# Head reciprocals spread by DMA through DRAM, score maxima turned by VectorE, in an attention and mixture-of-experts kernel

## The chip, the cores and the metric

The kernel runs on one core of one Trainium2 chip. The metric is the device time of one execution in microseconds. Five engines work in parallel, each on its own instruction stream in program order: TensorE (PE in the profile; its weight loads are listed as PEld), VectorE (DVE), ScalarE (ACT), GpSimd (POOL) and SyncE (SP), which here issues most DMA transfers. They wait for each other through semaphores only.

## The reference

One transformer block on `x` of 4 batches x 512 tokens x 128, in fp32. The first half is attention with 16 query heads of 64 and one shared key/value head:

```
x  = layernorm(x) ; xn = layernorm(x, g1, b1)
q  = (xn @ Wq).reshape(b, n, 16, 64) * 64**-0.5 ; k, v = split(xn @ Wkv)
attn = softmax(q @ k.T) ; out = attn @ v
x  = x_in + layernorm(out.reshape(b, n, 1024) @ Wo, g2, b2)
```

The second half is a mixture of 8 experts (two for each token, softmax gate, GELU with gating, hidden width 512), whose result is added to `x`.

## The kernel before

The program has two blocks. In the first, attention runs in 8 units of 8 heads (two units to a batch). `attention_schedule` writes one list of steps, each with a slot number; every engine walks the same list and issues what is its own. A slot is one `EXP` step: 128 keys by 512 queries of one head, so a head has 4 slots, a unit 32 and the whole attention 256.

- `MAX`: TensorE multiplies 128 queries by all 512 keys into one of two banks of `max_ps` (L1209), and VectorE takes the row maximum into `rowmax` (L1058). TensorE may write a bank again only when VectorE has read it: product k waits for maximum k-2.
- `SHIFT`, 17 times, mostly for 4 heads at once: the maxima must lie along the queries of one row. TensorE turns them with four transposes (L1216), ScalarE copies them with a factor of -1 into `mrow` (L1107), and two DMAs put them in row 64 of `q_hm` (L905). The step stands 5 slots ahead of the first `EXP` that needs it, at slots 11 and 27 of each unit (the first two heads apart).
- `EXP`: two products into `s_ps` (L1238, L1240; the second adds the negated maxima) and ScalarE's exponential into `prob` (L1134). `PV` (L1254) multiplies `prob` by `v`, 4 slots to a head, two heads at a time.
- The sum of each head: GpSimd adds its four `prob` tiles in two instructions, `fold` (L989, 128x1024) and `psums` (L995, 128x512), as soon as the head's last `EXP` is done. GpSimd also copies queries to `q_hm` (L969).
- After a unit: TensorE sums over the partitions into `sum_ps` (`SUM`, L787), ScalarE copies (`SUMS`), a DMA spreads the sums on 128 partitions (`SPREAD`), VectorE takes the reciprocals (`RECIP`, L718) and splits them in a high and a low part (L721, L722), two DMAs gather these into 16 rows of `rhl` (`GATHER`, L750). Then, for each of the 4 pairs of heads, `NORM`: TensorE multiplies a constant, `headsel`, by `rhl` (L797), which repeats each head's reciprocals on its 64 partitions of `sum_ps`, and VectorE multiplies that by `raw`, the unnormalized output, into `ao` (L731). `OUT` multiplies by `Wo` (L807). `NORM` stands at slots 14, 17, 19 and 22 of the next unit.

The second block does the experts. It opens with the last unit's `SPREAD` to `OUT`, mixed with the first expert tiles, while GpSimd sends rows to DRAM (L489) and then forms the low parts of the weights (L1356, `wl`).

Of the kernel before, what the change touches and what calls it, by code (L numbers as in the profile page):

```python
# [24 lines left out]
LOW_ROW = 32  # L25


def attention_schedule(units):
# [51 lines left out]
    for u in range(units):  # L80
        after = slots * (u + 1)
        if u < units - 1:
# [4 lines left out]
            for c in range(UP):  # L87
                place(after + NORM_AT[c], 5, "NORM", u, c)
                place(after + NORM_AT[c] + OUT_LAG, 5, "OUT", u, c)
# [28 lines left out]

SUM_AT = (-7, 5)
# [4 lines left out]
LAST_STEPS = (("SUMS", 0), ("SPREAD", 0), ("RECIP", 0), ("GATHER", 0), ("NORM", 0), ("NORM", 1), ("OUT", 0),  # L124
# [54 lines left out]
def bass_preln_mqa_moe_kernel(nc, x, ln1_g, ln1_b, wq, wkv, wo, ln2_g, ln2_b, gate_wT, gate_upT, downT,  # L179
# [16 lines left out]
    parts = nc.dram_tensor("parts", [TOP_K * T, P], F32).ap()  # L196

# [12 lines left out]
    with ExitStack() as whole:  # L210
# [64 lines left out]
        headsel = sb(whole, "headsel", [P, UP, P], F32R)  # L275
# [3 lines left out]
        halves = sb(whole, "halves", [P, 2, SPREAD], F32R)  # L279
        rhl = sb(whole, "rhl", [P, S], F32R)  # L280
# [403 lines left out]
        def load_rows(sp, k, dst):  # L684
# [49 lines left out]
        def tail_sync(sp, kind, u):  # L734
# [42 lines left out]
        def tail_tensor(pe, kind, u, a):  # L777

            b = u // 2
            if kind == "SUM":  # L780
                k = 2 * u + a
                sums_done(pe, 4 * (k + 1))
                if a == 0 and u >= 1:

                    pe.wait_ge(ao_ready, u * UP)
# [26 lines left out]
        tail_steps = [step for step in steps[last_pv:] if step[0] in ("RAW", *RECIP_STEPS, "NORM", "OUT")]  # L812
# [3 lines left out]
        with ExitStack() as att:  # L816
# [18 lines left out]
            rowmax = sb(att, "rowmax", [P, 2, TPB, 4])  # L835
            mrow = sb(att, "mrow", [4, 2, S], F32R)
# [11 lines left out]
            hs_raw = raw[:, RAW_SLOTS - 1, :].rearrange("p (u n) -> p u n", n=P)  # L848
# [16 lines left out]
            def shift_bank(n):  # L865


                return sum_ps if n == 0 else q_ps

# [3 lines left out]
            def _(sp):  # L873
# [10 lines left out]
                for half in range(2):  # L884
                    for part in range(2):
                        row = part * LOW_ROW + half * UH // 2
                        sp.dma_start(hs_raw[row:row + UH // 2, :, :],
                                     head_rows[half + 2 * part:P:32, :, :]).then_inc(hs_in, 16)
# [5 lines left out]
                for kind, u, a in steps:  # L894
                    tail_sync(sp, kind, u)
                    if kind == "SHIFT":
# [6 lines left out]
                        for h in range(0, heads, 2):  # L903
                            slot = (head + h) % Q_SLOTS
                            sp.dma_start(q_hm[DH:DH + 1, slot:slot + 2, :].bitcast(F32),  # L905
                                         mrow[h:h + 2, u % 2, :].bitcast(F32)).then_inc(mrow_in[u % 2], 16)
# [16 lines left out]
            def _(pool):  # L923
# [27 lines left out]
                for kind, u, a in steps:  # L951
# [12 lines left out]
                    if kind == "Q":  # L964
# [6 lines left out]
                        if k == 0:  # L971
                            link_pool(pool, nc.gpsimd.memset(headsel[:, :, :].bitcast(F32), 0.0))
# [758 lines left out]
```

## Time and profile before

| | us |
|---|---|
| median of 3 runs | 621.6 (621.18 to 623.62) |
| profiled execution | 620.37 |
| its span | 618.6 |
| TensorE busy | 579.3 (94%) |
| VectorE busy | 388.5 (63%) |
| GpSimd busy | 395.4 (64%) |
| ScalarE busy | 307.1 (50%) |

The span runs from the first to the last instruction that the profile shows; the execution's own time is 1.8 us more. Busy times of matmuls are modelled and overlap, so a busy TensorE is judged by the start times of its instructions. The granted clock of TensorE is a fraction of its full speed.

### The profile page before, as it was taken

Reading aid. Unit: us, or ns where it says so; the run is one execution under the profiler, and the core shown is the slowest. Engines: PE = TensorE matmul, PEld = TensorE weight load, DVE = VectorE, ACT = ScalarE, POOL = GpSimd, SP = SyncE. Lnnn points to the kernel's source line nnn. Section 1 sums busy time; section 2 is a strip of 40 time slices with the busy share of each in tenths; the row PEclk is TensorE's granted clock in tenths of the full one; section 3 lists DMA queues with packets and bytes.
Section 4 is the critical chain, followed back from the end, with each engine's and each line's share of the span. In section 5 each row is a group of like instructions: output and inputs, shape, how many; then the busy total and the mean of one; then the engine's idle time right before and its main releaser. Section 6 shows DMA issues by size and latency. Waiting matters only on the chain. (4 is left out here: it accounts for less than half of the span.)

```text
span 618.6 us, 8866 instructions
## 1 busy us (share of the span) xinstructions
PE 579.3 (94%) x2611; PEld 330.1 (53%) x2611; DVE 388.5 (63%) x792; ACT 307.1 (50%) x576; POOL 395.4 (64%) x329
## 2 busy tenths in 40 slices
PE   8799999999999998998999989999997979999990
PEld 6464555444554454454545535444443567888880
DVE  4967557656646878584567786975384468444443
ACT  2345646455546554463556445545635553455540
POOL 5457677658668855598598558959745934354331
PEclk9999999999999999798999999999999999999996
DMA  5111012010101200061000000000004400230005
GB/s 162 69 70 70 2 70 73 1 69 3 72 24 48 73 0 2 6 229 76 2 2 3 1 2 17 23 1 2 12 1 123 118 22 27 67 94 29 21 16 204
DMA packets 26990, 29.46 MB, mean 48 GB/s; under 512 B 7523, under 2 KB 18021, under 8 KB 26944
## 3 DMA queue, kind: packets, MB, share of 16 engines
q1 hardware_dynamic: 24672, 24.66, 12.3%
q0 software_dynamic: 2272, 4.24, 2.1%
q8 instruction: 23, 0.38, 0.3%
q14 instruction: 23, 0.19, 0.1%
HBM read 13.50 MB, written 15.32 MB: 47 GB/s over the span
## 5 line engine op out<-in xcount | busy, mean ns | idle before, releaser
L1134 ACT ACTIVATE prob<-s_ps 128x512 f32<-128x512 f32 x256 | 150.5, 598 | 177.0 <-PE s_ps L1240 175.1
L1058 DVE TENSOR_REDUCE rowmax<-max_ps 128x1 f32<-128x512 f32 x256 | 174.2, 690 | 101.4 <-PE max_ps L1209 99.1
L989 POOL TENSOR_TENSOR fold<-prob 128x1024 f32<-128x1024 f32 x63 | 149.8, 2377 | 94.5 <-ACT prob L1134 93.9
L1254 PE MATMUL pv_ps<-prob,v 128*64 128x512 f32 x512 | 139.0, 623 | 0.0
L1238 PE MATMUL s_ps<-q_hl,khh 128*128 128x512 f32 x256 | 118.5, 463 | 0.6 <-ACT prob L1134 0.6
L1209 PE MATMUL max_ps<-khh,q_hl 128*128 128x512 f32 x256 | 103.3, 409 | 7.7 <-DVE rowmax L1058 3.9
L1240 PE MATMUL s_ps<-q_hm,kly 65*128 65x512 f32 x256 | 102.3, 400 | 0.0
L1238 PEld LDWEIGHTS s_ps<-q_hl,khh 128*128 128x128 f32 x256 | 48.9, 191 | 79.5 <-ACT prob L1134 59.8
L995 POOL TENSOR_TENSOR psums<-fold 128x512 f32<-128x512 f32 x63 | 82.3, 1306 | 4.9
L1209 PEld LDWEIGHTS max_ps<-khh,q_hl 128*128 128x128 f32 x256 | 49.1, 192 | 27.3 <-DVE rowmax L1058 11.2
L1240 PEld LDWEIGHTS s_ps<-q_hm,kly 65*128 65x128 f32 x256 | 49.0, 191 | 8.9 <-issue 3.4
L1254 PEld LDWEIGHTS pv_ps<-prob,v 128*64 128x64 f32 x512 | 25.6, 135 | 46.1 <-issue 34.9
L489 POOL DMA_INDIRECT sorted_rows<-xr,place_i x32 | 34.2, 1068 | 21.4 <-issue 11.8
L1047 DVE TENSOR_TENSOR q_hl<-q_ps,q_hl 64x512 fp32r<-64x512 f32 x64 | 44.1, 689 | 5.9 <-ACT q_hl L1116 4.6
L1442 DVE TENSOR_TENSOR ha<-up_ps,gl 128x512 f32<-128x512 f32 x39 | 26.9, 690 | 30.8 <-PE up_ps L1569 22.7
L1591 PE MATMUL sum_ps<-wd,ht 128*128 x312 | 41.9, 277 | 4.3 <-DVE raw L1451 3.9
L1116 ACT ACTIVATE q_hl<-q_ps 64x512 fp32r<-64x512 f32 x64 | 37.6, 588 | 7.8 <-PE q_ps L1146 7.0
L1591 PEld LDWEIGHTS sum_ps<-wd,ht 128*128 128x128 f32 x312 | 37.9, 192 | 5.9 <-issue 5.9
L1403 POOL DMA_INDIRECT parts<-raw,psums x22 | 21.4, 973 | 30.3 <-DVE raw L1451 25.4
L731 DVE TENSOR_TENSOR ao<-sum_ps,raw 128x512 f32<-128x512 f32 x32 | 22.1, 691 | 28.9 <-PE sum_ps L797 28.9
L969 POOL TENSOR_SCALAR q_hm<-q_hl 64x1024 fp32r<-64x1024 f32 x32 | 33.4, 1044 | 6.7 <-ACT q_hl L1116 6.7
L1510 ACT ACTIVATE ht<-q_ps 128x512 f32<-128x512 f32 x39 | 23.3, 597 | 24.4 <-PE q_ps L1578 24.4
(230 smaller groups left out, 767.2 us busy)
## 6 DMA issues: line engine op xcount, KB each, us to landing
sorted_rows<-raw_w SPq DMA_DIRECT2D x36, 260.0 KB, 2.6
raw_w<-in_gate_upT SPq DMA_DIRECT2D x8, 512.0 KB, 8.3
wd<-in_downT SPq DMA_DIRECT2D x8, 256.0 KB
raw_w<-parts SPq DMA_DIRECT2D x8, 256.0 KB, 3.9
psums<-sorted_rows SPq DMA_DIRECT2D x22, 65.0 KB, 1.9
x<-in_x SPq DMA_DIRECT2D x4, 256.0 KB, 4.1
out<-x SPq DMA_DIRECT2D x4, 256.0 KB, 2.3
xs_first<-sorted_rows SPq DMA_DIRECT2D x15, 65.0 KB, 2.2
```

What stands on the lines that cost most here:

```text
L489: nc.gpsimd.indirect_dma_start(out=sorted_rows, out_offset=bass.IndirectOffsetOnAxis(ap=place_i[:, n, t:t + 1], axis=0), in_=xr[:, n, t, : ...
L989: nc.gpsimd.tensor_tensor(fold[:, :, :], prob[:, head % 4, 0:2, :], prob[:, head % 4, 2:4, :], ALU.add).then_inc(prob_folded, 1)
L995: nc.gpsimd.tensor_tensor(psums[:, head % SUM_SLOTS, :], fold[:, 0, :], fold[:, 1, :], ALU.add).then_inc(head_sum, 1)
L1047: nc.vector.tensor_tensor(q_hl[DH:P, h % Q_SLOTS, :], q_ps[DH * hd:DH * hd + DH, :], q_hl[0:DH, h % Q_SLOTS, :].bitcast(F32), ALU.subtract ...
L1058: nc.vector.tensor_reduce(rowmax[:, group % 2, it, i:i + 1], max_ps[:, k % 2, :], AX_X, ALU.max).then_inc(max_done, 1)
L1116: nc.scalar.activation(q_hl[0:DH, (2 * k + hd) % Q_SLOTS, :], q_ps[DH * hd:DH * hd + DH, :], ACT.Copy).then_inc(q_hi, 1)
L1134: nc.scalar.activation(prob[:, head % 4, jt, :], s_ps[:, k % 2, :], ACT.Exp, scale=SCALE).then_inc(exp_done, 1)
L1209: nc.tensor.matmul(max_ps[:, k % 2, :], q_hl[:, k // JT % Q_SLOTS, it * P:(it + 1) * P], khh[:, b % 2, :], start=True, stop=True).then_inc ...
L1238: nc.tensor.matmul(s_ps[:, k % 2, :], khh[:, b % 2, keys], q_hl[:, slot, :], start=True, stop=False)
L1240: nc.tensor.matmul(s_ps[:, k % 2, :], kly[0:DH + 1, b % 2, keys], q_hm[0:DH + 1, slot, :], start=False, stop=True).then_inc(score_mm, 1)
L1254: last = nc.tensor.matmul(pv_ps[DH * hd:DH * hd + DH, :], v[:, b % 2, jt, :], prob[:, head % 4, jt, :], start=(jt == 0), stop=(jt == JT - 1))
L1591: last = nc.tensor.matmul(down_ps[:, :], ht[:, k % 2, c * P:(c + 1) * P], wd[:, weights(k, DN, c * P, P)], start=c == 0, stop=c == FC - 1)
```

## The change

- `NORM` loses its product. `GATHER` writes the 128x32 reciprocals to a DRAM tensor, `recips`. Four new steps `CAST`, at slots 10.5, 10.5, 12 and 12, wait until that write has landed and read two heads' rows back, each row 64 times, into `over_sum`, which lies in SBUF (256 KB each). VectorE's `NORM` multiplies `over_sum` by `raw`, so that both of its inputs now lie in SBUF. The split in high and low parts, `headsel`, `rhl` and GpSimd's preparation of them go.
- `SHIFT` loses its transposes and ScalarE's copy. VectorE multiplies the maxima by -1 into `less_max` (128x16) and turns it with four 32x32 transposes into `mrow`. The two DMAs stay.
- In the second block, four `CAST` DMAs stand behind all loads of `wd`, and VectorE's four `NORM` behind the second `hidden`; the products that keep TensorE busy at the start of the block read other data.

```diff
             if kind == "RECIP":
                 dve.wait_ge(spread_in, 32 * (u + 1))
-                link(dve, nc.vector.reciprocal(rinv[:, :], spread[:, :]))
                 if u >= 1:
-                    dve.wait_ge(rhl_in, 32 * u)
-                link(dve, nc.vector.tensor_copy(halves[:, 0, :], rinv[:, :]))
-                nc.vector.tensor_tensor(halves[:, 1, :], rinv[:, :], halves[:, 0, :].bitcast(F32),
-                                        ALU.subtract).then_inc(recip_done, 1)
+                    dve.wait_ge(recips_out, 16 * u)
+                nc.vector.reciprocal(rinv[:, :], spread[:, :]).then_inc(recip_done, 1)
             if kind == "NORM":
                 k = u * UP + a
-                dve.wait_ge(norm_mm, k + 1)
+                dve.wait_ge(over_sum_in[a], 16 * (u + 1))
                 dve.wait_ge(raw_ready, k + 1)
...
-                nc.vector.tensor_tensor(ao[:, k % 2, :], sum_ps[:, :], raw[:, k % RAW_SLOTS, :],
+                nc.vector.tensor_tensor(ao[:, k % 2, :], over_sum[:, a, :], raw[:, k % RAW_SLOTS, :],
                                         ALU.mult).then_inc(ao_ready, 1)
...
             if kind == "GATHER":
                 sp.wait_ge(recip_done, u + 1)
+                sp.dma_start(recips[u].rearrange("(p c) -> p c", c=SPREAD), rinv[:, :]).then_inc(recips_out, 16)
+            if kind == "CAST":
+                sp.wait_ge(recips_out, 16 * (u + 1))
                 if u >= 1:
-                    sp.wait_ge(norm_mm, u * UP)
-                else:
-                    sp.wait_ge(consts_set, 1)
-                for part in range(2):
-                    sp.dma_start(rhl[part * LOW_ROW:part * LOW_ROW + UH, :].bitcast(F32),
-                                 halves[:, part, :].bitcast(F32)).then_inc(rhl_in, 16)
+                    sp.wait_ge(ao_ready, (u - 1) * UP + a + 1)
+                of_pair = recips[u, 2 * a * S:2 * (a + 1) * S].rearrange("(h q) -> h q", h=2)
+                sp.dma_start(over_sum[:, a, :],
+                             of_pair.unsqueeze(1).broadcast_to([2, DH, S])).then_inc(over_sum_in[a], 16)
...
-            if kind == "NORM":
-                k = u * UP + a
-                pe.wait_ge(rhl_in, 32 * (u + 1))
-                if k >= 1:
-                    pe.wait_ge(ao_ready, k)
-                nc.tensor.matmul(sum_ps[:, :], headsel[:, a, :], rhl[:, :], start=True,
-                                 stop=True).then_inc(norm_mm, 1)
...
+                    if kind == "SHIFT":
+                        head, heads = shift_heads[u]
+                        group, i = divmod(head, 4)
+                        cols = slice(i * JT, (i + heads) * JT)
+                        dve.wait_ge(max_done, (head + heads) * JT)
+                        if u >= 2:
+
+                            rows_came(dve, u - 2)
+                        link(dve, nc.vector.tensor_scalar(less_max[:, u % 2, cols], rowmax[:, group % 2, cols], -1.0, None,
+                                                          ALU.mult))
+                        for n in range(P // 32):
+                            part = slice(32 * n, 32 * n + 32)
+                            last = nc.vector.transpose(mrow[:, u % 2, part].bitcast(F32),
+                                                       less_max[part, u % 2, :].bitcast(F32))
+                        last.then_inc(mrow_ready, 1)
...
-                    if kind == "SHIFT":
-                        head, heads = shift_heads[u]
-                        pe.wait_ge(max_done, (head + heads) * JT)
-                        group, i = divmod(head, 4)
-                        for t in range(TPB):
-                            last = nc.tensor.transpose(shift_bank(u)[0:heads, t * P:(t + 1) * P],
-                                                       rowmax[:, group % 2, t, i:i + heads],
-                                                       ident[:, :])
-                        last.then_inc(shift_mm, 1)
```

On VectorE, early in the second unit, the kernel before has from the reciprocals to the first two `NORM` (the names in a row are what is written and what is read; x5 means five in a row):

```order
L718 RECIPROCAL rinv<-spread 128x32
L721 CAST halves<-rinv 128x32
L722 TENSOR_TENSOR halves<-rinv,halves 128x32
L1058 TENSOR_REDUCE rowmax<-max_ps 128x1 x5
L731 TENSOR_TENSOR ao<-sum_ps,raw 128x512
L1058 TENSOR_REDUCE rowmax<-max_ps 128x1 x2
L1047 TENSOR_TENSOR q_hl<-q_ps,q_hl 64x512 x2
```

The changed kernel has there on VectorE:

```order
L724 RECIPROCAL rinv<-spread 128x32
L1038 TENSOR_REDUCE rowmax<-max_ps 128x1 x2
L1048 TENSOR_SCALAR less_max<-rowmax 128x16
L1052 STREAM_TRANSPOSE mrow<-less_max 32x32 x4
L1038 TENSOR_REDUCE rowmax<-max_ps 128x1 x3
L732 TENSOR_TENSOR ao<-over_sum,raw 128x512
```

The split has gone, five small instructions stand between the second and the third maximum, and `NORM` reads `over_sum` in place of a bank of PSUM.

In the middle of the attention, in the unit in which a later batch's statistics (BN) are also taken, VectorE has before:

```order
L722 TENSOR_TENSOR halves<-rinv,halves 128x32
L1058 TENSOR_REDUCE rowmax<-max_ps 128x1 x2
L361 BN_STATS stats<-x 128x6 x4
L364 BN_AGGR moments<-stats 128x2 x4
L1058 TENSOR_REDUCE rowmax<-max_ps 128x1 x3
```

and after the change:

```order
L1038 TENSOR_REDUCE rowmax<-max_ps 128x1 x2
L1048 TENSOR_SCALAR less_max<-rowmax 128x16
L1052 STREAM_TRANSPOSE mrow<-less_max 32x32 x4
L363 BN_STATS stats<-x 128x6 x4
L366 BN_AGGR moments<-stats 128x2 x4
L1038 TENSOR_REDUCE rowmax<-max_ps 128x1 x3
```

The five instructions and the statistics now stand one behind the other ahead of the same three maxima.

## Rows read from the trace of the kernel before

**Rows 1.** The page, busy us of each engine (share of the span), instructions.
```profile
PE 579.3 (94%) x2611; PEld 330.1 (53%) x2611; DVE 388.5 (63%) x792; ACT 307.1 (50%) x576; POOL 395.4 (64%) x329
```

**Rows 2.** Busy us by engine in one stretch; then granted clock, DMA share, GB/s.
```profile
100.00:160.00 60.00, 60.00 (x244) 29.60 (x243) 37.76 (x63) 32.89 (x61) 41.13 (x28) 1.00 0.15 56
```

**Rows 3.** Timeline of TensorE: start, duration, line, operation; modelled ends.
```profile
99.80 0.60 PE L1216 MATMUL q_ps<-ident,rowmax 128*4 128x128 f32 x4
...
100.47 0.40 PE L1240 MATMUL s_ps<-q_hm,kly 65*128 65x512 f32 x1
...
103.46 0.50 PE L797 MATMUL sum_ps<-rhl,headsel 128*128 128x512 f32 x1
...
104.03 0.39 PE L1240 MATMUL s_ps<-q_hm,kly 65*128 65x512 f32 x1
...
106.99 0.50 PE L1238 MATMUL s_ps<-q_hl,khh 128*128 128x512 f32 x1
107.32 0.40 PE L1240 MATMUL s_ps<-q_hm,kly 65*128 65x512 f32 x1
```

**Rows 4.** Timeline: small VectorE instructions beside GpSimd; brackets give idle time before, releaser.
```profile
236.78 1.32 POOL L995 TENSOR_TENSOR psums<-fold 128x512 f32<-128x512 f32 x1
...
237.61 0.53 DVE L580 TENSOR_SCALAR picked<-cnt 128x32 f32<-128x32 f32 x1
...
240.77 2.37 POOL L989 TENSOR_TENSOR fold<-prob 128x1024 f32<-128x1024 f32 x1 [2.67 <-ACT prob L1134]
...
241.06 2.17 DVE L594 TENSOR_TENSOR of_pick<-pick,pr 128x64 f32<-128x64 f32 x1
...
399.65 2.83 DVE L657 TENSOR_TENSOR tile_j<-places,tile_j 128x9 f32<-128x9 f32 x1
...
404.07 0.50 PE L1209 MATMUL max_ps<-khh,q_hl 128*128 128x512 f32 x1 [0.96 <-DVE rowmax L1058]
```

**Rows 5.** Timeline around two SHIFT steps, at slots 11 and 27 of a unit.
```profile
99.34 2.38 POOL L989 TENSOR_TENSOR fold<-prob 128x1024 f32<-128x1024 f32 x1 [1.13 <-ACT prob L1134]
...
101.13 2.12 DVE L1058 TENSOR_REDUCE rowmax<-max_ps 128x1 f32<-128x512 f32 x3 [1.46 <-PE max_ps L1209]
...
102.13 0.39 PE L1209 MATMUL max_ps<-khh,q_hl 128*128 128x512 f32 x1
...
129.12 2.12 DVE L1058 TENSOR_REDUCE rowmax<-max_ps 128x1 f32<-128x512 f32 x3 [2.41 <-PE max_ps L1209]
```

**Rows 6.** Timeline around a SHIFT step with statistics beside it.
```profile
205.90 2.38 POOL L989 TENSOR_TENSOR fold<-prob 128x1024 f32<-128x1024 f32 x1 [0.82 <-ACT prob L1134]
...
206.47 0.86 DVE L361 BATCH_NORM_STATS2 stats<-x 128x6 f32<-128x128 f32 x4
...
207.69 2.12 DVE L1058 TENSOR_REDUCE rowmax<-max_ps 128x1 f32<-128x512 f32 x3
...
208.70 0.39 PE L1209 MATMUL max_ps<-khh,q_hl 128*128 128x512 f32 x1
```

**Rows 7.** The first SHIFT step: timeline of VectorE and ScalarE.
```profile
21.44 1.41 DVE L1047 TENSOR_TENSOR q_hl<-q_ps,q_hl 64x512 fp32r<-64x512 f32 x2
...
22.10 0.59 ACT L1107 ACTIVATE mrow<-sum_ps 2x512 fp32r<-2x512 f32 x1 [1.92 <-PE sum_ps L1216]
```

**Rows 8.** VectorE's NORM instructions (ns min/median/max) and what they waited for (us, times).
```profile
L731 DVE TENSOR_TENSOR ao<-sum_ps,raw x32: 680/692/693, 104.0 to 480.9; 128x512 f32<-128x512 f32 x32
...
  PE sum_ps L797: 28.9, 27
```

**Rows 9.** Stretches with idle TensorE, and one behind it; columns as in rows 2.
```profile
245.40:248.90 3.50, 1.49 (x6) 0.78 (x8) 3.41 (x6) 1.19 (x2) 0.44 (x2) 1.00 0.00 0
249.00:255.80 6.80, 6.80 (x22) 2.88 (x18) 2.75 (x8) 1.68 (x3) 3.21 (x2) 0.50 0.00 0
...
363.00:366.50 3.50, 1.54 (x6) 0.67 (x4) 3.41 (x6) 1.20 (x2) 0.43 (x2) 1.00 0.00 0
```

**Rows 10.** The second block: GpSimd's low weight parts in the timeline.
```profile
480.24 13.44 POOL L1356 TENSOR_TENSOR wl<-raw_w,wh 128x512 fp32r<-128x512 f32 x10
```

More of the change, by code:

```diff
@@ L24 @@
 SPREAD = 32
-LOW_ROW = 32
 def attention_schedule(units):
@@ L87, in attention_schedule @@
             for c in range(UP):
+                place(after + CAST_AT[c], 5, "CAST", u, c)
                 place(after + NORM_AT[c], 5, "NORM", u, c)
@@ L811, in bass_preln_mqa_moe_kernel @@
         last_pv = max(n for n, step in enumerate(steps) if step[0] == "PV")
-        tail_steps = [step for step in steps[last_pv:] if step[0] in ("RAW", *RECIP_STEPS, "NORM", "OUT")]
+        tail_steps = [step for step in steps[last_pv:] if step[0] in ("RAW", *RECIP_STEPS, "CAST", "NORM", "OUT")]
         assert all(step in tail_steps or step[0] in ("PV", "SUM") for step in steps[last_pv:])
@@ L834, in bass_preln_mqa_moe_kernel @@
             wvl = sb(att, "wvl", [P, DH], F32R)
-            rowmax = sb(att, "rowmax", [P, 2, TPB, 4])
-            mrow = sb(att, "mrow", [4, 2, S], F32R)
+            rowmax = sb(att, "rowmax", [P, 2, 4 * JT])
+            less_max = sb(att, "less_max", [P, 2, 32], F32R)
+            mrow = sb(att, "mrow", [32, 2, P], F32R)
             prob = sb(att, "prob", [P, 4, JT, S])
@@ L971, in _ @@
                         if k == 0:
-                            link_pool(pool, nc.gpsimd.memset(headsel[:, :, :].bitcast(F32), 0.0))
-                            link_pool(pool, nc.gpsimd.memset(rhl[:, :].bitcast(F32), 0.0))
-                            pool.wait_ge(hs_in, 64)
-                            for part in range(2):
-                                held = slice(part * LOW_ROW, part * LOW_ROW + UH)
-                                nc.gpsimd.tensor_scalar(headsel[held, :, :], hs_raw[held, :, :], 1.0, 1.0, ALU.mult,
-                                                        ALU.mult).then_inc(headsel_set, 1)
-                                pool.wait_ge(headsel_set, part + 1)
                             set_constants(pool)
@@ L1168, in _ @@
                         keep_busy(BUSY[kind])
-                    if kind in ("XT", "K", "V", "Q", "SHIFT", "YT", "X3T", "LOGIT", "RANK") and (kind, u) not in (("K", 0), ("SHIFT", 0)):
+                    if kind in ("XT", "K", "V", "Q", "YT", "X3T", "LOGIT", "RANK") and (kind, u) != ("K", 0):
                         if in_bank:
@@ L1371, in load_down @@
                                  downT[e].rearrange("(c p) n -> p c n", p=P)).then_inc(wd_in, 16)
[L1373 to L1379 removed]
+                tail_sync(sp, "SPREAD", last_unit, 0)
+                load_down(0)
+                load_down(1)
+                load_rows(sp, EARLY_ROWS, rows(EARLY_ROWS))
+                tail_sync(sp, "GATHER", last_unit, 0)
+                for e in range(2, E):
+                    load_down(e)
+                for c in range(UP):
+                    tail_sync(sp, "CAST", last_unit, c)
+                for k in range(EARLY_ROWS + 1, LIST_TILES[0]):
                     load_rows(sp, k, rows(k))
@@ L1457, in _ @@
                 low_gate_up(dve, 1, wl_ready)
-                tail_vector(dve, "NORM", last_unit, 0)
                 low_gate_up(dve, 2, wl_ready)
-                tail_vector(dve, "NORM", last_unit, 1)
                 hidden(1)
-                tail_vector(dve, "NORM", last_unit, 2)
-                tail_vector(dve, "NORM", last_unit, 3)
+                for c in range(UP):
+                    tail_vector(dve, "NORM", last_unit, c)
                 hidden(2)
@@ L1616, in up, with keep_busy @@
                     times(up_ps[:, k % 2, :], k, F).then_inc(up_mm, 1)
-                def keep_busy(times):
-                    for _ in range(times):
-                        nc.tensor.matmul(ht_ps[:, :], headsel[:, 0, :], headsel[:, :, :].rearrange("p k c -> p (k c)"),
-                                         start=True, stop=True)
-                keep_busy(4)
+                def keep_busy(width):
+                    nc.tensor.matmul(ht_ps[:, 0:width], ident[:, :], wof[:, 0:width // P, :].rearrange("p k c -> p (k c)"),
+                                     start=True, stop=True)
+                keep_busy(S)
                 turn_in(0)
-                keep_busy(2)
+                keep_busy(S // 2)
                 for e in range(E):
```

80 lines of the change are left out of this document (28 added, 52 removed).

## The prediction

> **What bounds the kernel now.** I read the page first: TensorE is busy 94% of the span, VectorE 63%, GpSimd 64% [rows 1]. Busy times of matmuls overlap by model, so I then took the stretches: between 100 and 160 us TensorE is busy 60.00 of 60.00 us at the full clock, while VectorE has 37.8 and GpSimd 41.1 [rows 2]. The timeline says the same by start times: the products follow each other at fixed distances, whatever the others do. So in the attention (to about 465 us) each product taken out is worth its distance to the next, as long as nobody makes TensorE wait. What can make it wait is VectorE: product k into `max_ps` waits for maximum k-2. So the questions are what leaves TensorE, and what the five new instructions and the new inputs of `NORM` do to VectorE's queue.
>
> **What is removed.** Behind a `PV` the next score product's partner L1240 starts 0.33 us after its L1238 (107.32 less 106.99). With a `NORM` product in front, it starts 0.57 us after that product's start (104.03 less 103.46), so `NORM` costs TensorE 0.24 us; with the four transposes in front 0.67 us (100.47 less 99.80), so a `SHIFT` costs 0.34 us [rows 3]. In the attention there are 28 `NORM` (four more come in the second block) and 17 `SHIFT`: 28 x 0.24 + 17 x 0.34 = 6.7 + 5.8 = 12.5 us saved. ScalarE's copies, GpSimd's preparation of `headsel` and VectorE's split go too; these engines have idle time there, so I count them at nothing. If that cover were gone (VectorE late), the split would give back about what the `SHIFT` instructions take; it stands at another place, so it does not help there.
>
> **What is added on VectorE: a wait for GpSimd.** The trace shows small VectorE instructions with all inputs and outputs in SBUF that last as long as a GpSimd instruction beside them. A 128x32 TENSOR_SCALAR takes 0.53 us and ends at 238.14, just after GpSimd's `psums` addition (236.78 + 1.32 = 238.10); a 128x64 TENSOR_TENSOR takes 2.17 us and ends at 243.23, just after a `fold` (240.77 + 2.37 = 243.14) [rows 4]. The first has one SBUF input, as `less_max` has; the second has two, as `NORM` now has. Maxima and additions that read PSUM keep their length.
>
> Each `SHIFT` stands right behind the last maximum of slot 11 or 27, and `fold` follows the exponential of the same slot. At 99.80 the transposes could start, because the maximum was ready; `fold` had started at 99.34 and ran to 101.72 [rows 3, 5]. So `less_max` gets in 0.4 us too late and ends at about 101.76. I find this order, by 0.2 to 1.1 us, at eleven of the seventeen steps. The four transposes are not in the trace. From below they cost nothing beyond the wait; from above 0.69 us each, as a full 128x512 instruction [rows 8]. I take 0.15 us each, since a 32-column instruction is nearest to the small ones here, whose work behind a wait is under 0.1 us: 0.6 us, VectorE free at 102.37.
>
> Place by place, with the maximum at 0.69 us:
> - Slot 11, no statistics, `fold` ahead: three steps. VectorE had been idle 1.46 us and took its next maximum at 101.13. Now it ends at 102.37 + 0.69 = 103.06, and the product that waits for it started at 102.13 [rows 5]. TensorE stands 0.93 us past its old time, 1.27 us with the 0.34 saved: 3 x 1.27 = 3.8 us.
> - Slot 11 with statistics: two steps. `fold` ends at 208.28, the transposes at 208.9, the statistics (1.22 us from 206.47 to 207.69) at 210.15, the maximum at 210.84, where the product started at 208.70 [rows 6]: 2.14 + 0.34 = 2.5 us, twice: 5.0 us.
> - Slot 27, six steps. VectorE was idle 2.41 us there, a microsecond more [rows 5], so that 1.27 becomes about 0.35: 2.1 us.
> - The first step. `mrow` came at 22.10 + 0.59 = 22.69 from ScalarE; VectorE is busy until 22.85 and would deliver at about 23.6 [rows 7]. The first `EXP` waits for it: 0.9 us.
> - The remaining five: nothing.
>
> A case in the trace bears this out: a VectorE wait of 2.83 us for GpSimd cost TensorE a gap of 0.96 us soon after [rows 4].
>
> `NORM` is kinder. It no longer waits for TensorE, which was 28.9 us over 27 of them, 1.07 us each, and its own time stays near 0.69 us [rows 8]. Against that stands a wait of up to one `fold`, 2.4 us, when it meets one. Laid over GpSimd's instructions, most of the 28 come out no later than before, a few later by up to 1.2 us: 1.9 us of waits in all, bounds 0 and 28 x 1.2 = 34 us, the low value because VectorE has over a third of its time free [rows 2].
>
> Sum so far: -12.5 + 3.8 + 5.0 + 2.1 + 0.9 + 1.9 = +1.2 us. The saving is spent in VectorE's queue.
>
> **The clock.** From 245.4 to 248.9 TensorE was busy 1.49 of 3.5 us, and from 249.0 to 255.8 it was granted 0.50, its level of 1.2 GHz; a like gap from 363.0 to 366.5 left it at 1.00 [rows 9]. The two gaps of 2.5 us are of this kind. A 3.4 us stretch at half speed loses 1.7 us. Bounds: none, and four of them (6.8 us, as after 249). I take one, 1.7 us.
>
> **The DMAs.** SyncE's queue gets, per unit, one write, a wait for it and four transfers of 256 KB. `SHIFT`'s DMAs stand between the `CAST` pairs and depend on `mrow`, which is late by 1.3 us at slot 11. The step stands five slots ahead of the `EXP` that it serves, some 8 us at 440 us for 256 slots; `mrow` would be there 2.6 us after 99.80, and two issues and a transfer fit in the rest. I count nothing, and 1 us for each of seven at worst.
>
> **The second block.** The `CAST` transfers queue behind 2 MB of `wd`, and I estimate the four `NORM` at 479 to 484, where the last one began at 480.9 before [rows 8]. There GpSimd works through ten `wl` subtractions, 13.44 us without a pause from 480.24 [rows 10], on which the first tiles with split weights wait. If `NORM` holds GpSimd off as GpSimd holds VectorE, each costs it up to 0.69 us; bounds 0 and 2.8 us. I take 1.5 us. No row here shows GpSimd held off by VectorE. The Trainium skill (SBUF — State Buffer, Who interferes with whom) says that the two share a port pair as an exclusive lock which the one that starts first keeps for its whole instruction; by it the term would be 2.8 us when all four collide.
>
> **Sum.** +1.2 + 1.7 + 1.5 = +4.4 us on the profiled execution's 620.4, that is 624.8. The median is 1.2 us above that execution, so 621.6 + 4.4 = 626.0 us.
>
> One page speaks for the change. The Trainium skill (VectorE: DVE Perf Modes, Rules for kernel authors) calls VectorE's transpose the fastest for 32x32, and gives 311 ns for a 128x128 bf16 one. With 0.31 us for each of my four, five gaps would be 0.64 us longer and the forecast 629.
>
> **The rivals.** A measurement tells about 0.5% (3.1 us) from no change.
> 1. *My forecast*, waits at the `SHIFT` steps that spend the saving, chance 0.45: 626.0, own range 622 to 632.
> 2. *The saving mostly stays*, 0.24. `less_max` comes first. ScalarE no longer copies the maxima, and VectorE reaches the step 0.2 to 1.1 us behind `fold`'s start: if it gets there ahead of `fold` in most units, GpSimd waits instead, which has slack. Then 3.8 + 5.0 + 2.1 shrink to about 2 us, no clock is lost: 621.6 - 12.5 + 2 + 0.9 + 1.9 + 1.0 = 615. It decides when `fold` starts later than the end of the last maximum in over half of the units. For it speaks that six of seventeen steps already go this way; against it that the order follows from the step list, slot after slot. Should `NORM` cost nothing either, 612.
> 3. *It evens out*, 0.20: waits of half my size and no clock loss, -12.5 + 7 + 1.5 = -4, or with one loss -2: 618.5 to 623.
> 4. *Worse*, 0.11: each of the seven gaps at slot 11 costs the clock, 7 x 1.7 = 11.9 in place of 1.7, or the late `mrow` adds its 7 us: 633 to 636.
>
> **How the numbers follow.** Rival 4 (0.11) and the part of my own range above 624.7 (0.36 of 0.45) are slower by over 0.5%; rival 2 (0.24) and the low end of 3 (0.02) are faster, below 618.5. That gives slower 0.47, same 0.27, faster 0.26. The range for 8 in 10 cuts off the ends of rivals 2 and 4: 612 to 633.
>
> **What would show it.** TENSOR_SCALAR of `less_max` at a mean well over 1 us (a minimum near 0.17), its end at `fold`'s; TensorE idle before max_ps products, released by `rowmax`, 12 us or more in all; transposes at 0.1 to 0.2 us; `NORM` between 0.7 and 3 us; a granted clock of 0.5 in new places behind the longest gaps; `wl` over 14 us. It is wrong if `less_max` is short in most steps, if the transposes cost more than 0.3 us each, or if TensorE's first `EXP` of a unit waits for a DMA.

## The result, and the profile after

The changed kernel takes 720.81 us (median of 4 runs, 720.35 to 721.71) against 621.39 us: a ratio of 1.159, 95% interval 1.156 to 1.162. The forecast was 626.0 with a range of 612 to 633. The sign of the likeliest case was right; the size was wrong by 95 us. The reason for most of it had been priced at 7 us at worst, in rival 4.

The page of the changed kernel, the lines that answer to [rows 1] and the groups with the largest waits:

```profile
PE 603.9 (84%) x2509; PEld 332.3 (46%) x2509; DVE 422.7 (59%) x862; ACT 298.0 (41%) x559; POOL 395.2 (55%) x325
...
L1215 PE MATMUL s_ps<-q_hl,khh 128*128 128x512 f32 x256 | 133.5, 521 | 44.8 <-DMA q_hm<-mrow 44.1
...
L1195 PE MATMUL max_ps<-khh,q_hl 128*128 128x512 f32 x256 | 108.1, 428 | 20.6 <-DVE rowmax L1038 16.8
...
L802 PE MATMUL y_ps<-ao,wof 128*128 128x512 f32 x64 | 41.6, 736 | 19.2 <-DVE ao L732 19.2
```

TensorE's share falls from 94% to 84%. It stands 44.1 us before `EXP` products because the maxima's rows (`q_hm<-mrow`) have not landed, 19.2 us before `OUT`, and 16.8 us before `MAX` products. The last is what the prediction was about. The first was its last condition for being wrong. The waits give how often (us in total, times, longest):

```profile
DVE ao L732 <- DMA over_sum<-recips: 45.3, 11, 10.6
PE s_ps L1215 <- DMA q_hm<-mrow: 44.1, 7, 9.1
...
PE y_ps L802 <- DVE ao L732: 19.2, 4, 9.9
...
PE max_ps L1195 <- DVE rowmax L1038: 16.8, 18, 2.7
```

One of the seven, in the timeline of the changed kernel from 100 us (SPq rows are SyncE's DMA issues: start, and how long the issuing took). It is the place of [rows 3] and [rows 5]:

```profile
101.90 1.11 SPq L752 DMA_DIRECT2D over_sum<-recips  x2
102.14 2.39 POOL L967 TENSOR_TENSOR fold<-prob 128x1024 f32<-128x1024 f32 x1 [1.14 <-ACT prob L1120]
102.31 2.25 DVE L1048 TENSOR_SCALAR less_max<-rowmax 128x16 fp32r<-128x16 f32 x1
...
104.60 0.84 DVE L1052 STREAM_TRANSPOSE mrow<-less_max 32x32 f32<-32x32 f32 x4
...
105.47 1.42 SPq L891 DMA_DIRECT2D q_hm<-mrow  x2
106.16 0.47 PE L1195 MATMUL max_ps<-khh,q_hl 128*128 128x512 f32 x1 [1.40 <-DVE rowmax L1038]
...
108.89 5.90 SPq L752 DMA_DIRECT2D over_sum<-recips  x2
...
115.37 0.79 PE L1215 MATMUL s_ps<-q_hl,khh 128*128 128x512 f32 x1 [6.14 <-DMA q_hm<-mrow]
```

Two things are to be seen. `less_max` starts 0.17 us behind `fold` and ends with it (104.56 and 104.53): the wait that I forecast, with the gap that I forecast (1.40 us, forecast 1.27). And two transfers of 4 KB, issued at 105.47 with two of 256 KB in flight before them, have landed only when the product starts at 115.37. What the DMA engines do meanwhile is in the windows of the same stretch (columns: PE, PEld, DVE, ACT and POOL busy, granted clock, mean share of the 16 DMA engines, GB/s):

```profile
104.00:106.00 2.00, 0.76 (x4) 0.30 (x2) 1.93 (x7) 1.44 (x3) 1.83 (x2) 1.00 0.13 51
...
108.00:110.00 2.00, 1.23 (x6) 0.66 (x4) 0.56 (x1) 0.60 (x1) 0.98 (x1) 1.00 1.05 395
...
112.00:114.00 2.00, 0.00 (x0) 0.00 (x0) 0.50 (x1) 0.00 (x0) 1.02 (x1) 0.75 0.13 43
114.00:116.00 2.00, 0.63 (x2) 0.53 (x3) 0.00 (x0) 0.00 (x0) 0.00 (x0) 0.50 0.13 49
116.00:118.00 2.00, 2.00 (x7) 0.59 (x5) 0.91 (x2) 1.35 (x3) 0.00 (x0) 0.50 0.13 50
```

With nothing but `CAST` in flight, the share is 0.13, which is 2 of 16, at 43 to 51 GB/s, while the same engines reach 395 GB/s between 108 and 110, when the loads of rows run. At 50 GB/s each 256 KB takes 5 us, and a unit has four. TensorE meanwhile drops to its lower clock (0.50, 1.2 GHz) and stays there into the work.

The 19.2 us ahead of `OUT` all lie in the second block, where TensorE takes up the four pairs of heads as their `CAST` transfers come in, 4.6 to 5.7 us apart:

```profile
564.45 2.08 PE L802 MATMUL y_ps<-ao,wof 128*128 128x512 f32 x2 [9.95 <-DVE ao L732]
570.14 2.08 PE L802 MATMUL y_ps<-ao,wof 128*128 128x512 f32 x2 [3.61 <-DVE ao L732]
574.76 2.08 PE L802 MATMUL y_ps<-ao,wof 128*128 128x512 f32 x2 [2.54 <-DVE ao L732]
579.90 2.08 PE L802 MATMUL y_ps<-ao,wof 128*128 128x512 f32 x2 [3.06 <-DVE ao L732]
```

### The profile page after: what moved, and what is told of

Its sections match the earlier page's. It is cut to its first block and busy times, and to the rows that moved or that the text cites. A ratio compares the mean times of both kernels' runs of the same rounds, so it can differ in the third digit from the quotient of the medians.

```text
span 719.2 us, 8703 instructions
## 1 busy us (share of the span) xinstructions
PE 603.9 (84%) x2509; PEld 332.3 (46%) x2509; DVE 422.7 (59%) x862; ACT 298.0 (41%) x559; POOL 395.2 (55%) x325
## 5 line engine op out<-in xcount | busy, mean ns | idle before, releaser
L1215 PE MATMUL s_ps<-q_hl,khh 128*128 128x512 f32 x256 | 133.5, 521 | 44.8 <-DMA q_hm<-mrow 44.1
L1231 PE MATMUL pv_ps<-prob,v 128*64 128x512 f32 x512 | 150.0, 668 | 0.0
L1195 PE MATMUL max_ps<-khh,q_hl 128*128 128x512 f32 x256 | 108.1, 428 | 20.6 <-DVE rowmax L1038 16.8
L1215 PEld LDWEIGHTS s_ps<-q_hl,khh 128*128 128x128 f32 x256 | 51.6, 202 | 153.7 <-ACT prob L1120 62.2
L1217 PE MATMUL s_ps<-q_hm,kly 65*128 65x512 f32 x256 | 107.1, 418 | 0.0
L973 POOL TENSOR_TENSOR psums<-fold 128x512 f32<-128x512 f32 x63 | 83.8, 1331 | 4.9
L1195 PEld LDWEIGHTS max_ps<-khh,q_hl 128*128 128x128 f32 x256 | 52.0, 203 | 45.3 <-issue 17.8
L732 DVE TENSOR_TENSOR ao<-over_sum,raw 128x512 f32<-128x512 f32 x32 | 30.3, 946 | 64.6 <-DMA over_sum<-recips 45.3
L1217 PEld LDWEIGHTS s_ps<-q_hm,kly 65*128 65x128 f32 x256 | 52.4, 205 | 11.7 <-issue 7.2
L802 PE MATMUL y_ps<-ao,wof 128*128 128x512 f32 x64 | 41.6, 736 | 19.2 <-DVE ao L732 19.2
L1231 PEld LDWEIGHTS pv_ps<-prob,v 128*64 128x64 f32 x512 | 26.8, 142 | 48.4 <-issue 37.8
L1026 DVE TENSOR_TENSOR q_hl<-q_ps,q_hl 64x512 fp32r<-64x512 f32 x64 | 44.1, 690 | 5.6 <-ACT q_hl L1103 4.1
L1103 ACT ACTIVATE q_hl<-q_ps 64x512 fp32r<-64x512 f32 x64 | 37.6, 587 | 12.5 <-PE q_ps L1132 11.6
```

The lines of the kernel that those rows point to most:

```text
L802: nc.tensor.matmul(y_ps[:, :], wof[:, c, :], ao[:, k % 2, :], start=c == 0, stop=c == PAIRS - 1).then_inc(out_mm, 1)
L973: nc.gpsimd.tensor_tensor(psums[:, head % SUM_SLOTS, :], fold[:, 0, :], fold[:, 1, :], ALU.add).then_inc(head_sum, 1)
L1026: nc.vector.tensor_tensor(q_hl[DH:P, h % Q_SLOTS, :], q_ps[DH * hd:DH * hd + DH, :], q_hl[0:DH, h % Q_SLOTS, :].bitcast(F32), ALU.subtract ...
L1103: nc.scalar.activation(q_hl[0:DH, (2 * k + hd) % Q_SLOTS, :], q_ps[DH * hd:DH * hd + DH, :], ACT.Copy).then_inc(q_hi, 1)
L1195: nc.tensor.matmul(max_ps[:, k % 2, :], q_hl[:, k // JT % Q_SLOTS, it * P:(it + 1) * P], khh[:, b % 2, :], start=True, stop=True).then_inc ...
L1215: nc.tensor.matmul(s_ps[:, k % 2, :], khh[:, b % 2, keys], q_hl[:, slot, :], start=True, stop=False)
```

## The experiments

Theory A was that two DMA engines carry each `CAST`. e1 to e3 test it; the question after them was what the two halves of the change cost by themselves, and e4 to e10 take them apart. The runs stand in the order of the argument. A difference between two kernels that ran beside different runs of the kernel before is good to about 3 us.

### e1: each CAST in two transfers

```diff
-                of_pair = recips[u, 2 * a * S:2 * (a + 1) * S].rearrange("(h q) -> h q", h=2)
-                sp.dma_start(over_sum[:, a, :],
-                             of_pair.unsqueeze(1).broadcast_to([2, DH, S])).then_inc(over_sum_in[a], 16)
+                for h in range(2):
+                    row = recips[u, (2 * a + h) * S:(2 * a + h + 1) * S].rearrange("(o q) -> o q", o=1)
+                    sp.dma_start(over_sum[h * DH:(h + 1) * DH, a, :],
+                                 row.broadcast_to([DH, S])).then_inc(over_sum_in[a], 16)
```

> Each CAST is made as two transfers, one for each head, whose pattern is 64 rows by 512 in place of 2 by 64 by 512; the bytes, the repeated row and all else stay. Theory A (the pattern with an outer dimension of 2 is carried by two of the sixteen DMA engines, share 0.13, so a 256 KB transfer takes 5 us, and the mrow transfers wait behind two of them): the DMA share during a CAST rises towards 1, TensorE's 44 us of waiting for q_hm<-mrow falls under 3 us, VectorE's 45 us for over_sum<-recips under 5 us, and the time comes to 626 us, what the prediction's other terms give. Theory B (reading one DRAM row 64 times is slow in itself): the time stays within 10 us of 720.

647.1 us, ratio 1.040 (1.032 to 1.049): 74 us come back by the shape of a transfer that moves the same bytes. Its windows have, for the same stretch:

```profile
104.00:106.00 2.00, 0.60 (x4) 0.20 (x3) 1.93 (x7) 1.26 (x3) 1.65 (x2) 1.00 0.54 168
```

And the answer on its tile `over_sum`:

```profile
DMA to landing us min/median/max: 2.7/3.0/4.8
```

Each half lands 3.0 us after its issue (median), TensorE's wait for `q_hm<-mrow` falls from 44.1 to 1.2 us, and four issues of `CAST` at 108.70 take 2.54 us where two took 5.90. A share of 0.13 could also be sixteen engines that are each busy an eighth of the time; the packets in the two traces speak against that. In both kernels a packet is a row of 2,048 bytes and mostly takes 84 ns. From 104.0 to 105.4 us the changed kernel never has fewer than two in flight, at 90% of the moments exactly two and else three; e1 has 6 to 17 (104.0 to 105.2). Theory A holds for the cause. Two of its numbers were missed: VectorE's wait for `over_sum` fell from 45.3 only to 10.0 us (expected under 5), and the time is 21 us above the 626 expected. Those 21 us are what e4 to e10 are about.

### e2: the same pattern, 128 different rows

```diff
-                             of_pair.unsqueeze(1).broadcast_to([2, DH, S])).then_inc(over_sum_in[a], 16)
+                sp.dma_start(over_sum[:, a, :].bitcast(F32), gate_upT[0:2, 0:DH, 0:S]).then_inc(over_sum_in[a], 16)
```

> Each CAST keeps its pattern of 2 by 64 by 512 but reads 128 different rows of the gate/up weights in place of two rows 64 times each; so over_sum holds other numbers, and the output is not the reference's. Theory A (the pattern decides): 720 us within 8, DMA share 0.13 during a CAST. Theory B (the repeated row decides): about 626 us.

717.0 us in one run, and the waits of the changed kernel:

```profile
DVE ao L732 <- DMA over_sum<-in_gate_upT: 47.4, 11, 10.0
PE s_ps L1213 <- DMA q_hm<-mrow: 45.6, 7, 9.6
```

That one row is read 64 times makes no difference that this one run shows. The pattern does it.

### e3: the maxima's rows ahead of all CAST

```diff
-CAST_AT = (10.5, 10.5, 12, 12)
+CAST_AT = (11.5, 11.5, 12, 12)
```

> The first two CAST steps move from slot 10.5 to 11.5, so that SyncE issues the mrow transfers of slot 11 ahead of all four CAST. Theory A with a queue in order: TensorE's wait for q_hm<-mrow falls from 44 us to under 10 us, the waits for over_sum stay or grow (the same 20 us of transfers for each unit, begun 4 us later), and the time falls by 20 to 40 us, to 680 to 700. If the slow transfers hold up the mrow rows whatever the order (the engines share them out), the time stays within 8 us of 720.

713.6 us in one run; I had expected 680 to 700. The wait for `mrow` has gone, and comes back in other rows of its waits:

```profile
DVE ao L732 <- DMA over_sum<-recips: 114.5, 27, 11.3
...
PE max_ps L1195 <- DVE rowmax L1038: 53.5, 26, 8.4
```

VectorE now stands in `NORM`, its maxima behind it, and TensorE waits for those (53.5 us, 16.8 in the changed kernel). Where the slow transfers stand in the queue hardly matters: 20 us of them per unit collide with one thing or another.

### e5: only VectorE's turn, NORM as before

The kernel before, with `SHIFT` of the changed kernel (`less_max` and four transposes in place of TensorE's transposes and ScalarE's copy) and nothing else.

> The kernel before with only the second part of the change: the maxima are negated and turned on VectorE; NORM keeps its product and the gather of before. The prediction's terms for this part: -5.8 us for the transposes, +3.8, +5.0, +2.1 and +0.9 us of waits, one loss of clock of 1.7 us: 621.4 + 7.7 = 629 us, range 622 to 634, less_max at a mean near 1.4 us. Rival (VectorE has room for it, the waits for GpSimd cost TensorE nothing): 621.4 - 5.8 = 615.6 us.

638.3 us, ratio 1.024 (1.016 to 1.031). Its `less_max` by duration (ns, least/median/longest):

```profile
L1072 DVE TENSOR_SCALAR less_max<-rowmax x17: 158/1720/2294, 21.8 to 449.6; 128x16 fp32r<-128x16 f32 x15, 128x8 fp32r<-128x8 f32 x2
```

TensorE's largest wait in it, which is 3.9 us in the kernel before:

```profile
PE max_ps L1220 <- DVE rowmax L1062: 17.1, 17, 2.7
```

And its windows at two gaps and behind three (PE busy, granted clock, DMA share, GB/s):

```profile
212.00:216.00 4.00, 1.38 (x6) 1.00 0.03 5
...
217.10:220.50 3.40, 3.40 (x10) 0.50 0.65 242
...
336.60:343.40 6.80, 6.05 (x13) 0.50 0.01 1
377.00:380.90 3.90, 1.77 (x7) 1.00 0.00 0
380.90:387.70 6.80, 6.80 (x24) 0.50 0.00 0
```

This half of the change alone costs 17 us (638.3 less 621.5, the kernel before beside it), where 7.7 were expected. The gaps are those of the prediction: 1.40 us three times, 2.72 twice, about 0.5 at four later steps. The clock is not: the mean granted clock is 0.962 (before 0.980). Half clock stands behind one of the three gaps of 1.40 us (3.4 us from 53.3 us on) and behind both of 2.72 (3.4 and 6.8 us). The 6.8 us from 380.9 on follow no gap of the change. They follow the one that [rows 9] shows from 363.0 on, where TensorE waits for VectorE's part in the choice of experts, and behind which the clock stayed at 1.00 before. Why it falls here and not there stays open.

### e7: the turn one slot earlier

```diff
-        place(FIRST_SHIFT_AT[n] if n < 2 else JT * head - lead + 1, 3, "SHIFT", n, 0)
+        place(FIRST_SHIFT_AT[n] if n < 2 else JT * head - lead, 3, "SHIFT", n, 0)
```

> The kernel of e5 (before, with the maxima turned on VectorE) with each SHIFT but the first two one slot earlier, at slots 10 and 26, so that less_max reaches VectorE before the fold of slot 11 or 27 has started. Theory (the time of e5 is less_max waiting for fold, the gaps that this makes on TensorE, and the clock lost behind them): less_max at a mean under 0.6 us in place of 1.34, TensorE's gaps before max_ps near the 8 us of before in place of 21, half clock near 27 us in place of 51, and 617 us, range 614 to 622. Rival (the five instructions cost this much wherever they stand): 632 or more.

637.6 us, ratio 1.030 (1.027 to 1.033): a miss. `less_max` did get ahead of `fold`, in 14 of 17 steps (the median is 165 ns):

```profile
L1072 DVE TENSOR_SCALAR less_max<-rowmax x17: 158/165/2324, 22.3 to 447.2; 128x16 fp32r<-128x16 f32 x15, 128x8 fp32r<-128x8 f32 x2
```

But two of the three that still wait are those ahead of the statistics, where the gaps are longest. One of them in the timeline of VectorE:

```profile
204.06 2.32 DVE L1072 TENSOR_SCALAR less_max<-rowmax 128x16 fp32r<-128x16 f32 x1
...
207.86 0.87 DVE L361 BATCH_NORM_STATS2 stats<-x 128x6 f32<-128x128 f32 x4
```

The windows of TensorE behind four gaps of the same kernel (columns as for e5):

```profile
209.00:216.00 7.00, 6.13 (x13) 0.51 0.41 154
...
253.00:260.00 7.00, 6.54 (x19) 0.54 0.01 2
...
332.00:339.00 7.00, 6.03 (x15) 0.51 0.01 1
376.00:386.00 10.00, 9.52 (x28) 0.52 0.00 0
```

Only the first and third of these stretches stand behind a wait of `less_max` ahead of statistics. The second is there in the kernel before too (249.0 to 255.8, [rows 9]); the fourth follows the gap that cost no clock before, as at 380.9 in e5. So taking the wait from most steps hardly moves the time: TensorE's wait for `rowmax` falls from 17.1 to 13.8 us, and the clock's loss stays near that of e5.

### e8: no negation, so no waiting instruction

```diff
-            less_max = sb(att, "less_max", [P, 2, 32], F32R)
...
-                        link(dve, nc.vector.tensor_scalar(less_max[:, u % 2, cols], rowmax[:, group % 2, cols], -1.0, None,
-                                                          ALU.mult))
...
-                nc.vector.memset(kly[DH:DH + 1, :, :].bitcast(F32), 1.0).then_inc(ones_set, 1)
+                nc.vector.memset(kly[DH:DH + 1, :, :].bitcast(F32), -1.0).then_inc(ones_set, 1)
```

e5, where the transposes read `rowmax` itself and the sign comes from the constant row of `kly` that multiplies it.

> The kernel of e5 without less_max: the maxima are turned as they are, straight from rowmax, and the row of ones in kly holds -1 in place of 1, so that the product subtracts them. It computes the same. Theory (the one instruction with the shared port waits; the transposes do not): TensorE's gaps before max_ps within 3 us of before's 8, and 617 us, range 614 to 622. Rival (the transposes themselves, 0.84 us for four, hold up the maxima): over 625.

616.9 us, ratio 0.9947 (0.9925 to 0.9969): 3 us faster than before, and some 20 us faster than e5 (21.5 by the medians, 18 by the ratios) for one 128x16 instruction less at each step. Its transposes:

```profile
L1072 DVE STREAM_TRANSPOSE mrow<-rowmax x68: 189/199/203, 22.8 to 428.9; 32x32 f32<-32x32 f32 x68
```

And TensorE's wait for maxima:

```profile
PE max_ps L1216 <- DVE rowmax L1061: 7.0, 10, 1.4
```

All 68 transposes take 189 to 203 ns, `fold` beside them or not; at 11 of the 17 steps they start while a `fold` runs. They read and write SBUF as `less_max` does, and don't wait for GpSimd. Of the 3.5 us that its profiled execution is ahead of before, 3.2 are clock: the 6.8 us at half clock that the kernel before has from 249 us on are not there. The seven runs of e8 (615.3 to 617.6) still lie below all ten of before beside them (618.0 and up).

### e10: e5 with the gaps filled

```diff
+                    if kind == "SHIFT":
+                        head = sum(shift_heads[u]) - 1
+                        if u in FILL:
+                            pe.wait_ge(*bank_read(*in_bank))
+                        for _ in range(FILL.get(u, 0)):
+                            nc.tensor.matmul(q_ps[:, :], q_hl[:, head % Q_SLOTS, 0:P],
+                                             khh[:, head // (2 * UH) % 2, :], start=True, stop=True)
...
+FILL = {2: 5, 4: 5, 5: 2, 6: 5, 8: 10, 9: 2, 12: 10, 13: 2}
```

> The kernel of e5_vector_turn_only (maxima turned by VectorE with the negation, NORM by product, 638.3 us), with products added on TensorE whose result nobody reads (q_ps, otherwise free there): 5 at the three SHIFT steps whose gap was 1.4 us, 10 at the two of 2.72 us, 2 at three of 0.53 us, 0.24 us each, 9.6 us in all, so that TensorE works through about the time that it stood still. Theory A: 10 us of e5's loss is the granted clock, which falls behind those gaps (50.8 us at half clock, before 26.9). The products lie in time that was idle, the gaps shrink by 8 us or more, half clock falls to 27 to 34 us, and the time goes down by 5 to 10 us: 628 to 633. Theory B: the clock falls for another reason, or with the work added: the half clock stays near 50 us, time 638 to 641. If the products delay VectorE's next maxima instead of hiding, gaps stay and the time rises towards 638 + 9.6 = 648.

634.5 us, ratio 1.019 (1.015 to 1.023), at a mean granted clock of 0.974 (e5 0.962). Its windows behind the two filled gaps with statistics, where e5 fell to 0.50:

```profile
216.00:224.00 8.00, 7.65 (x30) 1.00 0.38 138
336.00:344.00 8.00, 7.79 (x30) 1.00 0.00 1
```

41 products more, 9.8 us of work, and 4 us less time, a little short of the 5 to 10 expected. The intervals of the two ratios overlap, so the 4 us alone would prove little; that 9.8 us of added work did not make it slower says that the work lies in the gaps. The clock rose with it in every run: 0.974 to 0.975 in its four, 0.962 to 0.969 in those of e5.

### e6 and e4: the DMA way of NORM alone, and with the turn of e8

e6 is e1 with the turn of the kernel before (TensorE's transposes, ScalarE's copy). e4 is e1 with the edit of e8.

> Only the first part of the change, with CAST in two transfers: the reciprocals go through DRAM, the maxima are turned by TensorE and ScalarE as before (mrow lies in unused rows of q_hm for want of room). The prediction's terms: -6.7 + 1.9 + 1.5, so 618 us. By the difference of e1 and e5: 621.5 + 8.8 = 630. In e1 the second block shows 5.2 us in which TensorE waits for ao; with that alone and no other loss it is 621.5 - 6.7 + 5.2 = 620.

> The kernel of e1 (the whole change, CAST in two transfers) without less_max, in the manner of e8. e1 stands 8.8 us above e5. If the two parts of the change add up, this is e8 + 8.8, about 626; if NORM's waits for GpSimd only cost where less_max has already made VectorE late, it falls to 612 to 618, since the NORM products (6.7 us) are saved as well.

e6: 629.5 us, ratio 1.014 (1.009 to 1.019). e4: 627.4 us, 1.011 (1.007 to 1.015). The halves add up: the DMA way costs 9.5 us alone (e6 less the 619.9 of before beside it), 9 on top of e5 (e1 less e5), 10 to 11 on top of e8 (e4 less e8). Even with each transfer split in two it loses. In e6 7.0 us are TensorE's wait for `ao` in the second block; the rest of its loss no run takes apart. The longest wait of e4 is in the second block (its `POOL` row answers to [rows 10]):

```profile
477.98 5.37 SPq L753 DMA_DIRECT2D over_sum<-recips  x8
480.93 14.70 POOL L1330 TENSOR_TENSOR wl<-raw_w,wh 128x512 fp32r<-128x512 f32 x10
...
485.53 2.94 DVE L732 TENSOR_TENSOR ao<-over_sum,raw 128x512 f32<-128x512 f32 x2 [7.54 <-DMA over_sum<-recips]
...
486.86 4.71 PE L803 MATMUL y_ps<-ao,wof 128*128 128x512 f32 x6 [7.79 <-DVE ao L732]
...
489.07 1.07 DVE L732 TENSOR_TENSOR ao<-over_sum,raw 128x512 f32<-128x512 f32 x1 [0.60 <-PE y_ps L803]
```

The first `CAST` is issued at 477.98, behind `wd`, `NORM` starts at 485.53, and TensorE stands 7.79 us.

### e9: the last CAST ahead of wd

```diff
-                for e in range(2, E):
-                    load_down(e)
                 for c in range(UP):
                     tail_sync(sp, "CAST", last_unit, c)
+                for e in range(2, E):
+                    load_down(e)
```

> The kernel of e4_no_negation (reciprocals through DRAM in split transfers, maxima turned without the negation, 627.4 us), with the four CAST steps of the second block issued ahead of the last six loads of wd (1.5 MB) in place of behind them. In e4 the first CAST there was issued at about 479 us, and TensorE stood 7.8 us before its first y_ps product, waiting for ao. Theory A: that stall is the queue behind wd, which my prediction had not priced (it had 1.5 us for the whole second block). Then the wait falls to 1 us or less, and a stretch at half clock behind it goes too: 627.4 - 7 - 2 = 618 to 620. Theory B: TensorE waits there because NORM on VectorE and wl on GpSimd keep each other back (VectorE's NORM took 1.1 to 1.3 us there); then the order of the DMAs moves the stall by under 2 us and the time is 625 to 628. Either way a down product (sum_ps<-wd) may now wait for its weights: over 1 us of new wait there would say that wd has become late.

628.4 us, ratio 1.009 (1.006 to 1.012): no change from e4, whose interval it overlaps, though the wait did what theory A says. It fell from 7.79 to 1.75 + 0.97 us, against a new wait of 0.83 us for `wd`. Where the 5 us went stands first in the windows (PE busy, clock, share, GB/s) of e4:

```profile
483.00:487.00 4.00, 0.14 (x1) 0.60 0.85 217
487.00:491.00 4.00, 4.00 (x6) 0.54 0.28 70
491.00:496.00 5.00, 3.66 (x19) 1.00 0.25 59
```

Then in those of e9:

```profile
482.00:489.00 7.00, 6.04 (x10) 0.51 1.03 273
...
492.00:496.00 4.00, 3.48 (x6) 0.57 0.23 53
```

And in one row of e9's timeline:

```profile
531.00 1.15 PE L1566 MATMUL sum_ps<-wd,ht 128*128 x8 [1.91 <-DVE raw L1428]
```

In e4 a good part of the slow clock lay on idle time; in e9 it lies on work, with another stretch behind it. Against e4 the products of the first down tile start 3.2 us earlier, those of the second 1.7, and from the tile at 531 on, which waits 1.91 us for VectorE, none. What keeps VectorE there stays open: its late instruction is shown as waiting for "remote", which names no engine.

### What adds up

For each kernel: the product time taken out or put in, at the prediction's prices (`SHIFT` 0.34, `NORM` 0.24, 32 of them; e10's products 0.24); the idle time of TensorE between its matmul records from 14 us on (21.8 us before); and the time lost to the clock, (1 - mean granted clock) x span (0.020 x 618.6 = 12.4 us before).

| kernel | products | idle | clock | sum | span less 618.6 |
|---|---|---|---|---|---|
| changed | -13.5 | +74.7 | +58.8 | +120.0 | +100.6 |
| e1 | -13.5 | +21.6 | +18.6 | +26.7 | +26.8 |
| e5 | -5.8 | +13.4 | +11.8 | +19.4 | +19.0 |
| e7 | -5.8 | +10.7 | +10.4 | +15.3 | +14.8 |
| e10 | +4.0 | +5.2 | +4.1 | +13.3 | +14.2 |
| e8 | -5.8 | +4.4 | -3.2 | -4.6 | -3.5 |
| e6 | -7.7 | +10.3 | +9.0 | +11.6 | +10.4 |
| e4 | -13.5 | +11.6 | +12.7 | +10.8 | +8.1 |
| e9 | -13.5 | +8.9 | +12.1 | +7.5 | +8.6 |

The three terms give every span within 3 us, but for the changed kernel, where much of the slow clock lies on idle time and is counted twice. The saving is there in all of them. In the eight kernels with 5 us or more of added idle time, the clock took 0.8 to 1.4 us for each of these. That is a sum over a kernel and no price of a single gap: e8 has 4.4 us more of idle time and 3.2 less of lost clock, and two of the three gaps of 1.40 us in e5 cost no clock. The clock's term also holds the end of the span, behind TensorE's last product, where a low clock costs nothing: 5.6 us before, and 0.1 to 2.4 us more than that in the others.

## Why the prediction was wrong, by its own steps

- **The DMAs, "I count nothing, and 1 us for each of seven at worst": the step that failed.** The seven places were right; they cost 44.1 us, 6.3 each, and in the second block the late `over_sum` cost 19.2 more. I took a `CAST` for one transfer of 256 KB like others on the page, and didn't ask how its access pattern is shared out. e1, e2 and e3 show it: same bytes in rows of 64, 74 us less; other data, no change; another order, 7 us. The Trainium skill (DMA: Bandwidth & Descriptors, Why a DMA increments its semaphore by 16 and not by 1) says that a transfer gets the largest number of engines up to 16 that divides the slowest dimension of both its sides. The pattern of `CAST` is 2 x 64 x 512 on the DRAM side: two engines. By that rule, the trace agrees (0.13 = 2/16, and two packets in flight); it could have been read off the diff.
- **Waits at SHIFT, 3.8 + 5.0 + 2.1 + 0.9: right in place and size.** In the changed kernel the gaps with no statistics are 1.40 us at three steps (forecast 1.27), with statistics 2.72 at two (2.5), at slot 27 0.53 at three (0.35 at six), and `less_max` ends with `fold`. At the first step e5 loses 1.0 us (forecast 0.9), but not by a wait for `mrow`: TensorE stands 1.50 us for VectorE's `q_hl` and 1.10 for a maximum. e8 shows the cause: take out the instruction that waits, and the step is a gain. The transposes took 0.20 us each, not 0.15 (four 0.84). The Trainium skill's 0.31 us (VectorE: DVE Perf Modes, The three transpose paths) is for a 128x128 bf16 one and was farther off.
- **The clock, 1.7 us, bounds 0 to 6.8: mis-sized.** In e5, where nothing but the turn is changed, it took 11.8 us; in e1 18.6. Without the end of the span these are 10.3 and 17.1. I priced one stretch of 3.4 us because a like gap in [rows 9] had gone free. In e5 the half-clock stretches behind the new gaps come to 13.6 us, which costs 6.8, the upper bound; the rest came where I had not looked, 6.8 us of half clock behind an old gap and 3.4 us in the second block. Rival 4 came nearest, at a chance of 0.11, but its mechanism ("each of the seven gaps at slot 11 costs the clock", 11.9 us) isn't what happened: in e5 two of the three gaps of 1.40 us cost nothing, and 11.9 meets 11.8 by luck. Its 633 to 636 is the case nearest to e1, and still 11 us short.
- **NORM, saved 0.24 each and waits of 1.9 us: saving right, waits about right in the attention.** In e1 `NORM` takes 1.07 us on the mean, up to 2.67, where it had 0.69 [rows 8]. In e6, where the turn is as before, TensorE's idle time ahead of `MAX` products is 9.3 us (7.7 before): 1.6 us of waits, forecast 1.9.
- **The second block, 1.5 us, bounds 0 to 2.8: right for what I named, blind for the rest.** `wl` grew from 13.44 [rows 10] to 14.70 us in e4, 1.3 us, and a single `NORM` took 1.07 in place of 0.69: GpSimd and VectorE hold each other off. But the transfers behind 2 MB of `wd` made TensorE stand 7.79 us, which I had not priced, though the sentence ahead said that they queue. e9 shows that undoing this wait alone wins nothing.
- **Sum.** With the DMA fault mended (e1) the terms gave +4.4 us and the chip +26.8: 17 of the 22 us are clock by the table (15 without the end of the span), and 5.2 us are TensorE's wait for `ao` in the second block. Of the forecast's error of 95 us, the DMAs' shape is 74 and the clock in e1 17. One sum of the rivals doesn't come out: rival 3's -4 and -2 give 617.6 and 619.6, not 618.5 to 623.

## What to carry to other kernels

Before pricing a DMA by its bytes, look at the outermost dimension of both access patterns: a broadcast or a pair of rows put there first can leave 14 of 16 engines idle, and the first to suffer are the small transfers behind it. When an engine's own work is the bound, price new gaps twice, once as idle time and once as clock (0.8 to 1.4 us for each here, in sum, though single gaps went free), and look for the instruction that causes it: here one 128x16 multiplication by -1, whose sign could go into a constant, cost some 20 us. A saving on the busy engine holds only if what replaces it doesn't wait: of the whole change, the transposes on VectorE without the negation are the part worth keeping (0.995 of the time before, 0.9925 to 0.9969).

## What the runs showed that I had not expected

- A 256 KB transfer with outermost dimension 2 runs at 43 to 51 GB/s on a DMA share of 0.13; as two transfers of 64 rows it reaches 168 GB/s in the same 2 us, and lands in 3.0 us.
- SyncE is held up too: two issues of such transfers took 5.90 us, four of the split ones 2.54.
- A 32x32 fp32 transpose on VectorE takes 0.20 us and isn't held off by GpSimd's `fold` (189 to 203 ns over 68), while a 128x16 multiplication between the same memories takes up to 2.32 us beside it (e7; 0.16 alone). The Trainium skill (SBUF — State Buffer, Who interferes with whom) ties the wait to two-port modes and to two SBUF inputs; a multiplication with one input that waits would have to be the first, and no run here shows its mode; the transposes would be neither.
- 9.8 us of products whose result nobody reads, put where TensorE stood still, cost no time (e10 634.5, e5 638.3) and raised the mean granted clock from 0.962 to 0.974.
